# Statements of the second and third phase's half steps in another order on four engines

## The reference

```python
x = emb[tokens] + pos                      # phase 1: a tower of 4 layers
for l in range(4):
    n = layernorm(x); h = scan(a, n @ B); x = x + h @ C + n @ D
    x = x + gelu(layernorm(x) @ w1 + b1) @ w2 + b2
x = layernorm(x)                           # phase 2: one layer, 16 heads of 16
e = exp(-gamma * scale * max(dist2(q, k), 0)) * causal;  x = x + (e @ v) @ Wo
x0 = x; x = layernorm(x)                   # phase 3: two layers, 8 heads of 64
for l in range(2):
    q, k, v = split(shift_token(x) @ wqkv)
    q, k = rotary(l2norm(q)), rotary(l2norm(k))
    o = softmax(mask(8 * q @ k.T)) @ v     # window of 128 tokens, causal
    x = x + o @ wo
    h = layernorm(shift_token(x)) @ w1 + b1
    x = x + (a * gelu(g)) @ w2 + b2        # a, g = split(h), 682 wide
return x0 + x
```

## Time and profile before

| | us |
|---|---|
| median of 3 runs | 1275.08 (1273.28 to 1277.85) |
| profiled execution, its own time | 1278.31 |
| its span | 1276.4 |
| TensorE busy | 1209.8 |
| VectorE busy | 984.7 |
| ScalarE busy | 860.2 |
| GpSimd busy | 621.2 |

### The profile page before, as it was taken

How to read it: one execution, slowest core, us unless ns; L and a number is a source line. 1 busy time by engine, 2 the same in 40 slices (tenths; PEclk the granted TensorE clock), 3 DMA queues, 4 the chain that set the end, 5 groups by cost and what they waited for, 6 DMA issues and landing times.

```text
span 1276.4 us, 26138 instructions
## 1 busy us (share of the span) xinstructions
PE 1209.8 (95%) x8899; PEld 1028.5 (81%) x8899; DVE 984.7 (77%) x2624; ACT 860.2 (67%) x1989; POOL 621.2 (49%) x678
## 2 busy tenths in 40 slices
PE   5999999999999999799978799999999999999998
PEld 3799988988888989577756567888888888888898
DVE  5767676666667777789878988888888888888754
ACT  2455766675556556689964668778777777777764
POOL 6523441361145243455434568556655567556543
PEclk9899999999999999899989999999999999999999
DMA  7400010001000000300110002000100000000001
GB/s 172 115 2 15 2 66 0 14 33 33 0 8 1 1 1 1 77 10 18 58 54 17 1 5 95 6 5 6 48 3 6 22 6 13 22 17 18 22 10 42
DMA packets 39615, 33.25 MB, mean 26 GB/s; under 512 B 16774, under 2 KB 36178, under 8 KB 39506
## 3 DMA queue, kind: packets, MB, share of 16 engines
q1 hardware_dynamic: 38610, 29.74, 7.7%
q0 software_dynamic: 768, 2.10, 1.0%
q10 hardware_dynamic: 128, 0.04, 0.0%
HBM read 25.84 MB, written 4.19 MB: 24 GB/s over the span
## 4 chain that ended last, share of the span: by engine, by line
PE 45%; DVE 6%; issue 3%; POOL 2%; ACT 2%; DVEq 0%; ACTq 0%; POOLq 0%
PE w_ps_p L1914 3%; PE w_ring L1975 3%; PE w_ring L1976 3%; PE w_ring L1873 3%; PE w_ring L1977 3%; PE w_ring L1875 3%; PE w_ring L1874 3%; PE w_ps_a L1932 2%; PE w_ring L1987 2%; PE a_ps L925 2%; PE w_ps_d L1907 2%; PE w_ps_d L1904 2%; PE w_ring L1891 2%; PE w_ring L1988 2%; PE w_ring L1991 1%
## 5 line engine op out<-in xcount | busy, mean ns | idle before, releaser
L392 ACT ACTIVATE t_gf<-t_ps_f,t_fb_cur 128x512 f32<-128x512 f32 x128 | 87.9, 687 | 159.8 <-PE t_ps_f L298 156.6
L542 DVE TENSOR_TENSOR t_g_lo<-t_gf,t_g_hi 128x512 fp32r<-128x512 f32 x128 | 93.3, 730 | 69.3 <-ACT t_g_hi L394 68.9
L311 PE MATMUL t_ps_o<-t_w_hi,t_g_hi 128*128 128x256 f32 x512 | 144.6, 282 | 0.1
L312 PE MATMUL t_ps_o<-t_w_lo,t_g_hi 128*128 128x256 f32 x512 | 143.0, 279 | 0.0
L313 PE MATMUL t_ps_o<-t_w_hi,t_g_lo 128*128 128x256 f32 x512 | 142.9, 279 | 0.0
L695 POOL TENSOR_TENSOR t_rs<-t_ve,t_neghalf 128x4 f32<-128x4 f32 x32 | 40.9, 1277 | 159.8 <-DVE t_ve L503 158.2
L296 PE MATMUL t_ps_f<-t_nh,t_w_hi 128*128 128x512 f32 x256 | 102.6, 401 | 1.5 <-DVE t_nl L518 0.8
L2988 POOL TENSOR_TENSOR w_m<-w_m 128x512 f32<-128x512 f32 x64 | 84.2, 1316 | 36.9 <-DVE w_m L2631 36.8
L298 PE MATMUL t_ps_f<-t_nl,t_w_hi 128*128 128x512 f32 x256 | 100.3, 392 | 0.0
L297 PE MATMUL t_ps_f<-t_nh,t_w_lo 128*128 128x512 f32 x256 | 100.0, 391 | 0.0
L311 PEld LDWEIGHTS t_ps_o<-t_w_hi,t_g_hi 128*128 128x128 f32 x512 | 96.2, 188 | 4.1 <-issue 0.9
(11 more groups left out here) (369 smaller groups left out, 4285.0 us busy)
## 6 DMA issues: line engine op xcount, KB each, us to landing
t_raw<-in_L_tok_w SPq DMA_DIRECT2D x8, 1024.0 KB, 5.4
out<-X SPq DMA_DIRECT2D x14, 256.0 KB, 2.2
raw<-in_L_ffn_wqkv SPq DMA_DIRECT2D x2, 1536.0 KB, 6.9
raw<-in_L_ffn_w SPq DMA_DIRECT2D x4, 640.0 KB, 4.8
w_raw_o<-out SPq DMA_DIRECT2D x8, 256.0 KB, 2.8
w_xs<-X SPq DMA_DIRECT2D x14, 127.0 KB
w_raw<-in_L_ffn_w SPq DMA_DIRECT2D x2, 640.0 KB
t_raw_d<-in_L_tok_D SPq DMA_DIRECT2D x4, 256.0 KB
```

The source lines that it names most:

```text
L311: pe.matmul(out, g_hi[:, j % 4, tok], w2_hi[:, j, :], start=(j == 0 and t % 2 == 0), stop=False, skip_group_check=True)
L312: pe.matmul(out, g_hi[:, j % 4, tok], w2_lo[:, j, :], start=False, stop=False, skip_group_check=True)
L392: act.activation(gf[:, j % 2, :], ps_f[:, j % 2, :], ACT.Gelu, bias=fb_cur[:, j:j + 1]).then_inc(pf_free, 1)
L542: dve.tensor_tensor(g_lo[:, j % 4, :], gf[:, j % 2, :], g_hi[:, j % 4, :].bitcast(F32), ALU.subtract).then_inc(g_split, 1)
```

## The change

Statements within `half` are put in another order on TensorE, ScalarE, VectorE and GpSimd, in phase 2 and in phase 3. Where an early return ended the last half step, each statement behind it has the condition `h != M + 1` instead. No computation, wait or buffer is added or taken away, but for some branches that never ran. The diff, cut to the lines that matter; first TensorE (end of phase 2, then phase 3):

```diff
                     distances(b, 0, 3)
-                if turn_first:
-                    turn_first()
-                if real(c):
-                    values(c, 2, 2)
                 if real(a):
...
                     project_qk(a, 0, 0)
+                if real(c):
+                    values(c, 2, 2)
+                if turn_first:
+                    turn_first()
                 if real(b):
                     pe.wait_ge(relu_done, 8 * b + 1)
...
+                if real(g) and real(d):
+                    if real(c):
+                        pe.wait_ge(S["qt_done"], 2 * c + 2)
+                    pe.wait_ge(S["gated"], FC * g + 4)
+                    hidden_in(g, 4, 0, 3, "a_full")
                 if real(d):
                     turn_p(H * d + 5)
...
                     scores(NU * c + 0)
-                if real(g):
-                    hidden_out(g, 1, 1)
+                if real(d):
+                    values(NU * d + 2)
...
                     project_out(e, 0)
-                if real(d):
-                    values(NU * d + 2)
                 if real(c):
                     scores(NU * c + 1)
```

ScalarE, from `gelu` to the end of the half step, new order:

```diff
                     gelu(f, 5, 2)
-                    if real(b) or real(c):
-                        act.preload_act_table_set("natural_log_exp_and_others")
...
+                if real(b):
+                    root(b, 1)
+                if real(d) and h != M + 1:
+                    output_hi(NU * d + 3)
                 if h == 13:
                     hi_2(1)
...
                 if real(c):
                     probabilities(H * c + 4)
-                if real(b) and h != 1:
+                if real(b) and h != 1 and h != M + 1:
                     keep_values(b, 0, 3)
-                if real(c):
+                if real(a) and h != 1 and h != M + 1:
+                    spread(a, 0)
+                if real(c) and h != M + 1:
                     probabilities(H * c + 5)
...
+                if real(b) and h != M + 1:
+                    turned(b, 0, 1, 1)
+                if real(f) and (real(b) or real(c)):
+                    act.preload_act_table_set("natural_log_exp_and_others")
```

```diff
+                if real(b) and h != M + 1:
+                    inverse_root(b, 0)
                 if real(c):
                     turned_p(H * c + 0)
...
+                if real(f) and h != M + 1:
+                    gated(f, 0, 1)
+                if real(d) and h != M + 1:
+                    output_lo(NU * d + 3)
+                if real(f) and h != M + 1:
+                    gated(f, 1, 1)
+                if real(b) and h != M + 1:
+                    inverse_root(b, 1)
...
                     inverse_sums(NU * c + 3)
+                    turned_p(H * c + 5)
                     output_lo(NU * c + 1)
-                    turned_p(H * c + 5)
```

GpSimd:

```diff
                     scale_k(b, 1)
-                if h == 5:
-                    x0_root(3)
-                if 0 <= f < M - 1:
-                    hidden_lo(f, 0)
-                if 0 <= f < M - 1:
-                    hidden_lo(f, 1)
-                if h == 8:
-                    lo_qkv(2)
                 if real(c):
                     scale_p(NU * c + 2)
                 if 0 <= f < M - 1:
+                    hidden_lo(f, 0)
+                    hidden_lo(f, 1)
...
                 if real(e):
                     add_bias(e)
...
+                if h == 8:
+                    lo_qkv(2)
...
+                if real(d) and h != M:
+                    rstd(d)
...
+                if h == 12:
+                    lo_2(1)
                 if h == 11:
                     lo_1(1, 1)
```

More of the change, by code:

```diff
@@ L2167, in half @@
                     project(b, 1, 1, 3, "k_full")
+                if real(d):
+                    turn_p(H * d + 6)
+                if real(g):
+                    hidden_out(g, 2, 1)
                 if real(f):
@@ L2527, in half @@
                     probabilities(H * c + 1)
+                if h == 8:
+                    hi_qkv(1, "k_full")
+                if h == 4 and h != M + 1:
+                    hi_2(0)
+                if h == 1:
+                    spread(1, 0)
+                if real(d):
+                    output_hi(NU * d + 2)
                 if real(b):
@@ L2842, in half @@
                     add_attention(e, 0)
-                    upper_stats(e)
+                if real(c):
+                    inverse_sums(NU * c + 0)
+                    soft(H * c + 2)
+                    soft(H * c + 3)
+                if h == 2 and h != M + 1:
+                    x0_variance(2)
+                if real(d):
+                    turned_p(H * d + 7)
+                    output_lo(NU * d + 2)
+                if real(c):
+                    soft(H * c + 4)
+                if h == 1 and h != M + 1:
+                    split_in(a, 0)
+                if h == 5:
+                    x0_variance(3)
+                if real(c):
+                    inverse_sums(NU * c + 1)
+                if 0 <= g < M - 1:
+                    hidden_lo(g, 5)
+                if real(b) and h != M + 1:
+                    inverse_root(b, 0)
+                if real(c):
+                    turned_p(H * c + 0)
+                if real(b):
+                    clamp(b, 1)
                 if h == 6:
@@ L2890, in half @@
-                if h == 2:
-                    x0_variance(2)
-                if real(c):
-                    turned_p(H * c + 2)
-                if h == 2:
-                    fills()
-                if real(a) and h != 1:
-                    split_in(a, 0)
-                if h == 0:
-                    x0_variance(1)
-                if h == 0:
-                    x0_norm(1)
-                if real(c):
+                if real(c) and h != M + 1:
+                    turned_p(H * c + 2)
```

376 lines of the change are left out of this document (160 added, 216 removed).

## The result

The changed kernel takes 1308.0 us (median of 4 runs, 1305.2 to 1313.6) against 1276.0 for the kernel before on the same chip: ratio 1.026, interval 1.022 to 1.030. The forecast was 1268, so it has the wrong sign and misses by 40. The profiled execution has a span of 1303.3; before it was 1276.4.

The account below looks back on a forecast made before the run. TensorE, busy 95% of the span, was taken to bound the full third phase, VectorE part of its fill, with three engines nearly full in the second phase; terms summed to -7.2, 1275.1 to 1267.9 us, range 1256 to 1282.

Parts of the forecast that it names:

- (e): GpSimd's scale_p ahead of hidden_lo and lo_qkv(2): the three waits for pr go, -2.8 us.
- (b): Step 1 of the third phase's fill: split_in directly behind rotate shortens the wait for the second al, -0.7 us.
- (c): Step 2 of the fill: x0_variance(2) moves up into VectorE's idle time, -2.0 us, between 0.4 and 2.5 won.
- (d): Step 3 of the fill: turn_p and values far apart, x0_norm(2) behind the chain, -1.0 us, bounds 0 and 3.
- (g): TensorE's own cost of order: scores always followed by values or transposes, 0.1 over nine full steps, -0.9 us.
- (h): ScalarE's late table preload: two extra loads a step in 12 steps, mostly covered, +2.4 us, bounds 0 and 30.8.
- signs of being right: No pr wait at 906 and 1193, second al wait about 2.4, full steps 35.5 us, two more table loads a step.
- (j): Rest of the full step: no new wait in most steps, no DMA issue moved on any queue, +0.5 us in all.
- slower rival: ScalarE's late tables and VectorE's blocked operations make a wait in every full step, at 1.5 a step 1283; chance 0.17.
- (a): End of the second phase: values(c, 2, 2) ahead of turn_first fills the wait for al, -1.0 us, bounds 0 and 1.6.
- (i): Second phase otherwise: the same instructions in another order on nearly full engines, 0 us, bounds -3 and +3.
- (f): The 1.80 us wait at 1082.62 and the half clock behind it: output_lo ahead of the second inverse_root, -1.7 us.

Follow-up runs that it names:

- b_scale_p: The kernel before with GpSimd's scale_p(NU*c+2) alone moved up, ahead of hidden_lo(f, 0), lo_qkv(2) and x0_root(3): 1272.3 us.
- b_pool3_spf: The kernel before with GpSimd's new third-phase order, and SyncE's shifts ahead of load_1(1) and load_h: 1276.0 us.
- sp_first: The changed kernel with SyncE's queue alone reordered, shift(5) ahead of load_1(1) and shifts 9 to 13 ahead of load_h: 1282.4 us.
- best2: spf_p2_table with VectorE's inverse_root(b, 0) behind turned_p(c, 0) and add_output(g, 1) in steps 8, 9 and 13 alone: 1273.5 us, ratio 0.9974 to the kernel before.
- b_phase2: The kernel before with the second phase's order alone, on all four engines, taken from the changed kernel: 1278.3 us.
- spf_root_late: sp_first with VectorE's inverse_root(b, 0) behind turned_p(c, 0) and add_output(g, 1) in all steps, as in the kernel before: 1279.2 us.
- spf_p2_table: The changed kernel with shifts first in SyncE's queue, the old second-phase order, and the table set loaded directly behind gelu: 1275.7 us.
- best: spf_p2_table with VectorE's inverse_root(b, 0) late in steps 7, 8 and 12 alone, one too early; column 9 37.4 us, total time not stated.

## Why the prediction was wrong

Right, in whole or in part:
- (e), 2.8: no wait for `pr`, and 2.8 alone in b_scale_p. With the rest of GpSimd's new order (b_pool3_spf) it isn't a net gain.
- (b), (c), (d), 3.7 together: the second `al` wait is 2.52 (forecast 2.4), as (b) said. But column 0 is 4.2 shorter in the changed kernel and only 1.7 to 1.8 in sp_first and best2. Of the 4.2, 2.4 lie between `turn_in(0)` and the first projection (5.43 before, 3.04 after), where one of the two `values` is gone and the clock isn't halved; part of the rest is the clock too: the step after `turn_in(1)` had 1.00 in place of 0.93. (d) failed: the waits for `pt` in the fill didn't shrink (4.4 in 5 from 668 to 820, 4.4 in 4 before), and those of `scores` for VectorE's maxima `mx` grew from 1.6 to 5.2. All waits of TensorE that the view lists there sum to 18.1, and to 17.9 before.
- (g): full steps of 35.5, 0.1 less.
- (h), +2.4: the loads counted right, the cost 1.9 to 3.9.

Of the signs of being right, no `pr` waits, a second `al` wait near 2.4, full steps of 35.5 and two more loads a step came out, and the time was 40 off all the same: none of them looks at the steps in which the loss lies. The signs of being wrong came out too: columns 5, 6 and 10 to 12 are above 36, a wait recurs at L1893 (L1891 before), though only 2.8 us in 6, and half steps of the second phase left 17.4.

Wrong:
- (j), the failed step: "No DMA issue is moved on any queue; a shift starts when `x_mid` is set". SyncE's own list was unchanged, and I took that for its timing. A queue in order is moved by what releases the entries ahead. The diff moves `lo_qkv(2)` and `add_bias(e)`, and both release a load that stands ahead of a shift. In before's trace the air was to be read: 15 us for `load_1(1)`, against a statement that goes behind `add_bias`, which in that step started at 915.94, 13.7 after it, and goes later itself; and 1.5 us for `load_h(11)`, against the `add_sin` and the `scale_p(NU*b+0)`, with its wait for VectorE's sums, that `add_bias` goes behind. `shift(9)` was already 3.0 behind its L2683 there. Cost 25.6.
- (j) again: the blocked operations, which my slower rival had for the full step, came in the few steps with weight splits, and the victim was `add_output`, not `turn(1, 0, 3)`. 3.2 by spf_root_late; between spf_p2_table and best2 4.4 from turn_in(0) to the end (613.6 and 609.2), 2.2 by the medians.
- (a): -1.0 taken, not won. The wait of 1.62 for `al` is still there, ahead of the first projection at 667.54, and the one ahead of `turn_in(0)`, for VectorE's normalization, grew from 0.77 to 1.52:

```profile
664.50 0.63 PE L1861 MATMUL w_ring<-w_ident,X 128*128 128x128 f32 x4 [1.52 <-DVE X L2606]
```
- (i): 0 taken. b_phase2 has the moves of (a) too, so its 2.7 lost are (a) and (i) together, against the -1.0 forecast for both: 3.7 off. Either size lies within the bounds of (i).
- (f): 1.7 taken, not won. Column 10 is 40.3 in sp_first and 39.1 in best2, the same as in the kernel before; 37.5, in spf_root_late, is the least of any run. The other remedies passed the wait on to the next reader.

The queue's 25.6, 3.7 for (a) and (i), 3.2 for the blocked operations, 1.7 for (f) and 1.0 for (h), by the medians on sp_first, are 35 of the 40. Another 0.9 is that the kernel before took 1276.0 beside it and not 1275.1, and 1.9 that (b) to (d) brought 1.8 in place of 3.7. These prices come from medians of different kernels, each uncertain by 2 or 3 us, so that they nearly add up is partly luck; no run separates what is left. Of the rivals none named a held transfer; the slower one had the right sign and the wrong mechanism, and that its 1283 is near sp_first's 1282.4, the time without the held queue, is chance: full steps didn't grow by 1.5, which it was worked out from.

## What to carry to other kernels

When a statement moves on one engine, list the semaphores that it sets and follow each to every queue that waits for it, also those the diff doesn't touch; then compare the shift with the air between that entry and the next one behind it. Put transfers on which the critical path hangs ahead of loads for later, if their semaphores come at similar times. And move one thing at a time: one statement was worth as much as the new orders of four engines.

## What the runs showed of the hardware

The stretches at half clock don't lie at the same places in each execution. Runs best and best2 are the same up to the seventh step of the third phase, yet `turn_in(0)` starts at 659.8 in one and 663.5 in the other; from 500 to there the granted clock is 0.96 and 0.94. The 12 times of best2 lie in two groups, 1268.9 to 1269.9 and 1273.2 to 1275.3, and its profile is of the second. The 29 times of the kernel before beside it have two groups too, 1272.4 to 1275.0 and 1276.1 to 1279.5. So an effect of 3 us in a median needs the columns of a trace beside it.
